# Halving the tails of a four-network graph kernel: fourth network in halves, jump bias and row bits moved into the layers, idle products at the seams

## The reference, cut to what matters

```python
# first network: attention
h = relu(layernorm(x)); s = si[:, :, None] + sj[:, None, :] + a_b
e = exp(s) * adj; x += einsum('bij,bjc->bic', e / e.sum(2), h)
# second network: rows are thinned one after another, then three layers
adj_d = dilate(adj, mask)
def sage(x, Wr, Wx, b):
    out = (einsum('bij,bjd->bid', adj_d, x) / deg) @ Wr + x @ Wx + b
    return out / max(norm(out), 1e-12)
h1 = bn(relu(sage(h, ...)));  h2 = bn(relu(sage(h1, ...)));  h3 = bn(relu(sage(h2, ...)))
x += (concat(h1, h2, h3) * mf) @ Wl + bl      # jump, with the bias bl
# "fourth network" in the words of the change: normalised adjacency
h = relu(layernorm(x)); x += einsum('bnm,bmo->bno', d * (adj + I) * d, h @ W2) + bias
# last network
h = relu(layernorm(x)); x += relu(einsum('bji,bjd->bid', adj > 0, h) @ U / deg)
```

## Time and profile before

| | us |
|---|---|
| median of 3 runs | 1387.33 (1386.73 to 1391.0) |
| the profiled execution | 1389.99 |
| its span, first to last instruction | 1388.3 |
| mean granted TensorE clock | 0.924 |
| PE busy | 1176.5 (85%) |
| DVE busy | 814.0 (59%) |
| ACT busy | 614.8 (44%) |
| POOL busy | 83.1 (6%) |

### The profile page before, as it was taken

One profiled execution on the slowest core, in us unless ns is written; L12 is line 12 of the kernel. 1 busy time (PEld: TensorE's weight loads), 2 busy tenths in 40 slices (PEclk: granted clock), 3 DMA queues, 4 the chain that ended last, 5 costly groups with the idle time before them and its releaser, 6 DMA issues. The chain is left out here.

```text
span 1388.3 us, 28432 instructions
## 1 busy us (share of the span) xinstructions
PE 1176.5 (85%) x10649; PEld 1028.9 (74%) x10649; DVE 814.0 (59%) x2816; ACT 614.8 (44%) x1510; POOL 83.1 (6%) x64
## 2 busy tenths in 40 slices
PE   4798879886488989988959999599997299998998
PEld 4798856554367777777859999599997298987554
DVE  4799577778755555565532343334454457766883
ACT  5699637766644444554222323313333223222541
POOL 2012000000000000000000000000000324310000
PEclk9899989975599999999979999799999589999999
DMA  9866000000045654456304563136675235671931
GB/s 324 284 245 243 32 2 3 2 3 2 2 182 215 240 220 188 187 200 239 123 31 166 199 242 123 44 146 228 237 296 226 85 120 223 264 275 77 409 119 46
DMA packets 75950, 225.35 MB, mean 162 GB/s; under 512 B 4960, under 2 KB 23584, under 8 KB 75808
## 3 DMA queue, kind: packets, MB, share of 16 engines
q1 hardware_dynamic: 75088, 223.40, 42.7%
q10 hardware_dynamic: 720, 0.07, 0.0%
HBM read 185.70 MB, written 37.75 MB: 161 GB/s over the span
## 5 line engine op out<-in xcount | busy, mean ns | idle before, releaser
L1332 PE MATMUL lay_acc<-lay_z,k_keepadj 128*128 128x128 f32 x1024 | 117.0, 275 | 0.0
L1332 PE MATMUL lay_acc<-lay_z,k_otheradj 128*128 128x128 f32 x1024 | 116.6, 275 | 0.0
L1332 PEld LDWEIGHTS lay_acc<-lay_z,k_keepadj 128*128 128x128 f32 x1024 | 115.6, 192 | 0.0
L1332 PEld LDWEIGHTS lay_acc<-lay_z,k_otheradj 128*128 128x128 f32 x1024 | 115.5, 192 | 0.0
L1416 DVE TENSOR_TENSOR lay_o<-lay_ring,k_vec 128x512 f32<-128x512 f32 x32 | 22.1, 692 | 135.3 <-PE lay_ring L1325 135.3
L1371 ACT ACTIVATE lay_junk<-lay_o 128x128 bf16<-128x128 f32 x128 | 37.7, 295 | 136.2 <-DVEq L1439 136.2
L1081 ACT ACTIVATE fuse_dist<-fuse_prank,k_kb 128x512 f16<-128x512 f32 (+2 forms) x96 | 55.3, 576 | 76.4 <-PE fuse_prank L974 73.0
L319 PE MATMUL att_acc<-att_rhs,att_adjT 128*128 128x130 f32 x512 | 63.2, 290 | 17.5 <-DMA att_adjT<-in_adj_cols 11.3
L319 PEld LDWEIGHTS att_acc<-att_rhs,att_adjT 128*128 128x128 f32 x512 | 62.5, 205 | 18.1 <-POOLq L276 18.1
L974 PE MATMUL fuse_prank<-k_fore,k_T 128*128 128x128 fp8e5 (+3 forms) x416 | 63.4, 291 | 11.0 <-PEq L140 7.5
L319 PE MATMUL att_acc<-att_rhs,k_keepadj 128*128 128x130 f32 x512 | 61.7, 285 | 7.9 <-DVEq L429 3.3
(11 more groups left out here) (268 smaller groups left out, 2623.2 us busy)
## 6 DMA issues: line engine op xcount, KB each, us to landing
k_keepadj<-in_adj_cols SPq DMA_DIRECT2D x28, 1024.0 KB, 8.1
k_keepadj<-keptT SPq DMA_DIRECT2D x12, 2048.0 KB, 10.5
k_otheradj<-keptT SPq DMA_DIRECT2D x12, 2048.0 KB, 11.5
att_adjT<-in_adj_cols SPq DMA_DIRECT2D x16, 1024.0 KB, 6.7
k_otheradj<-in_adj_cols SPq DMA_DIRECT2D x16, 1024.0 KB, 10.6
keptT<-k_keepadj SPq DMA_DIRECT2D x16, 1024.0 KB, 5.1
keptT<-k_otheradj SPq DMA_DIRECT2D x16, 1024.0 KB, 4.4
k_keepadj<-in_adj_cols SPq DMA_DIRECT2D x8, 2048.0 KB, 10.9
```

Source lines behind the costliest of these rows:

```text
L1332: mm = t.matmul(acc[i % 2][k][:, ib % HB, :], adjT[i % 2][:, jb, ib * P:(ib + 1) * P], zz[i % 2][:, jb, :], start=(jb == 0), stop=(jb == N ...
```

## The change

What it does, in the order of the phases:

- Attention: one semaphore per graph's features. The features of the third and fourth graph are loaded behind the first and second adjacency.
- Keep stage and layers: `outputs`, `squares`, `weights`, `rectified`, the transposes and (in the layers) the statistics work by halves of four tiles; the semaphores count halves.
- Layers: for the last graph, the transposes of the graph before stand between the two halves of its sums, not behind them. Behind the last sums the chain of the last graph runs half by half.
- Idle products (`keep_busy`): products of a 128x128 bf16 by a 128x512 fp8 operand whose result nobody reads, 26 at the end of the keep stage, 12 at the start and 18 at the end of each layer, 12 and 22 at the start of the fourth network.
- Row bits are made in layers 1 and 2; the fourth network has none.
- The jump bias is added by GpSimd in layer 2, two tiles at a time.
- Fourth network: `eT` for the entry beside `hT`; entry, projections, update, statistics, scales, normalisation, transposes, turned copies and support in halves; the degrees behind the first normalisation; `entry(b + 2)` ahead of the turned copy.

```diff
-ROWS_OF_LAYER = {1: [], 2: [(g, jb) for g in (0, 1) for jb in range(8)], 3: [(g, jb) for g in (2, 3) for jb in range(8)]}
+ROWS_OF_LAYER = {1: [(g, jb) for g in (0, 1) for jb in range(8)], 2: [(g, jb) for g in (2, 3) for jb in range(8)]}
@@ attention_phase
-                    sp.dma_start(x_rows(i), graph(A["x"], order[i])).then_inc(x_first[i] if i < 2 else x_rest, 16)
+                    sp.dma_start(x_rows(i), graph(A["x"], order[i])).then_inc(x_loaded[i], 16)
...
                 for i in range(2):
                     for c in range(NC):
                         load_adjacency(i, c)
-                for i in range(2, B):
+                    load_x(i + 2)
+                for i in range(4, B):
                     load_x(i)
@@ fuse_phase
+                    if b == B:
+                        keep_busy(t, K, pmask[0][:], 26)
...
-                def squares(b):
-                    act.wait_ge(out_ready, b + 1)
-                    for ib in range(NB):
+                def squares(b, half):
+                    act.wait_ge(out_ready, b * 2 + half + 1)
+                    for ib in range(half * HB, (half + 1) * HB):
...
+                        if ib == HB - 1:
+                            dve.drain().then_inc(out_ready, 1)
...
+def keep_busy(t, K, out, count):
+
+    for _ in range(count):
+        t.matmul(out, K["ident16"][:], K["fore8"][:, 0:HALF], start=True, stop=True)
@@ layer_phase, TensorE
+                keep_busy(t, K, acc[1][1][:].rearrange("p e d -> p (e d)"), 12)
...
+                    if i == B - 1:
+                        project(i - 1, "r0")
+                        project(i - 1, "r1")
                     if i < B:
                         sums(i, 1)
                         pe.drain().then_inc(adj_used, 1)
-                    if i > 0:
+                    if i == B:
+                        project(i - 1, "r0")
+                        pe.wait_ge(acc_free, B - 1)
+                        keep_busy(t, K, acc[B % 2][0][:].rearrange("p e d -> p (e d)"), 18)
+                        project(i - 1, "r1")
+                    elif 0 < i < B - 1:
@@ layer_phase, ScalarE
+                    if i == B:
+                        for half in range(2):
+                            squares(i - 1, half)
+                            rectified(i - 1, half)
+                            turned_copy(i - 1, half)
@@ layer_phase, GpSimd and VectorE
+                for i in range(B if final else 0):
+                    pool.wait_ge(x_added, 2 * i + 2)
+                    for tile in range(seq[i] * NB, (seq[i] + 1) * NB, 2):
+                        x = K["X"][:, tile:tile + 2, :]
+                        g.tensor_tensor(bl[:], along_tiles(K["vec"][:, V_BL, :], 2), along_features(K["mask"][:, tile:tile + 2], D),
+                                        ALU.mult)
+                        pool.drain()
+                        g.tensor_tensor(x, x, bl[:], ALU.add)
+                        pool.drain()
...
+                    if i == B:
+                        for half in range(2):
+                            outputs(i - 1, half)
+                            weights(i - 1, half)
+                        for half in range(2):
+                            batch_statistics(i - 1, half)
@@ gcn_phase, TensorE
+                keep_busy(t, K, tp[:, 0:HALF], 12)
                 project(0, 0)
-                turn(0)
+                keep_busy(t, K, acc[1][:].rearrange("p e d -> p (e d)"), 22)
+                turn(0, 0)
+                turn(0, 1)
                 project(0, 1)
@@ gcn_phase, ScalarE
+                entry(0)
+                for b in range(B):
+                    normalise(b)
                     if b == 0:
-                        act.wait_ge(sem["cols_ready"], 1)
-                    else:
-                        act.wait_ge(sem["pr_ready"], b * 2)
...
+                        act.wait_ge(deg_ready, 1)
+                        a.activation(dinv[:], dw[:, 1, :], ACT.Sqrt).then_inc(dinv_ready, 1)
+                    if b > 0 and b + 1 < B:
+                        entry(b + 1)
+                    turned_copy(b)
+                    if b == 0:
+                        entry(1)
@@ gcn_phase, VectorE
+                def normalise(b):
+
+                    update(b, 0)
+                    means(b, 0)
+                    update(b, 1)
+                    scales(b, 0)
+                    means(b, 1)
+                    scales(b, 1)
...
+                normalise(0)
+                degrees()
+                support(0)
+                for b in range(B):
+                    if b + 1 < B:
                         normalise(b + 1)
```

More of the change, by code:

```diff
@@ L1586, in body @@
-                    if not last:
+                        pe.wait_ge(loaded[b % 2], 32 * (b // 2))
+                    if b > 0:
+                        pe.wait_ge(sums_read, 2 * b - 1)
+                    sums(b, range(0, 4)).then_inc(sums_ready, 1)
+                    if b > 0:
+                        pe.wait_ge(sums_read, 2 * b)
+                    sums(b, range(4, 6))
+                    if b + 1 < B:
+                        turn(b + 1, 0)
+                        turn(b + 1, 1)
+                    sums(b, range(6, 8)).then_inc(sums_ready, 1)
@@ L1611, in body, with entry @@
-                def body(b, par, last):
-                    if not last:
-                        prepare(b + 1)
-                prepare(0)
-                for b in range(B):
-                    body(b, b % 2, b == B - 1)
-                norm_root(nc, act, K, w, B)
-                norm_apply(nc, act, lambda t: K["X"][:, t, :], h[:], w, B, sem["h_ready"])
+                def entry(b):
+                    for half in range(2):
+                        if b == 0:
+                            act.wait_ge(cols_ready, 1)
+                        else:
+                            act.wait_ge(pr_ready, projected(b - 1, 0, half))
+                        sl = slice(half * HALF, (half + 1) * HALF)
+                        a.activation(eT[:, sl], turned(T8, b)[:, sl], ACT.Identity, scale=c["col"][:, 4:5], bias=c["col"][:, 5:6])\
+                            .then_inc(eT_ready, 1)
@@ new lines, in normalise @@
+                def normalise(b):
+                    s_ = w["stat"]
+                    for half in range(2):
+                        ts = of_half(half)
+                        act.wait_ge(w["mean_ready"], 2 * b + half + 1)
+                        a.activation(s_[:, 0, ts], w["pair"][:, ts, 1], ACT.Sqrt, bias=K["eps"][:, 0:1]).then_inc(w["std_ready"], 1)
+                        act.wait_ge(w["scale_ready"], 2 * b + half + 1)
+                        for t in range(half * HB, (half + 1) * HB):
+                            last = a.activation(h[:, t, :], K["X"][:, b * NB + t, :], ACT.Relu, bias=s_[:, 2, t:t + 1],
+                                                scale=s_[:, 1, t:t + 1])
+                        last.then_inc(h_ready, 1)
```

374 lines of the change are left out of this document (179 added, 195 removed).

## The result

The median is **1349.66 us** (1348.63 to 1351.07, 4 runs) against 1388.39 (1386.73 to 1391.0, 4 runs) for the kernel before beside it: ratio 0.971, 95% interval 0.9692 to 0.9728. The profiled execution took 1351.07 us with a span of 1349.4; before it was 1389.99 and 1388.3. So 38.9 us went, where the forecast had 51.1. Cut at the same events in both traces, the span falls into these stretches (us). An aggregate is VectorE's instruction that makes mean and variance out of the statistics, the first one behind a seam; the sums are the products with the adjacency.

The account below looks back on a forecast made before the run. TensorE bounds the layers' insides (busy 99%); at five seams every instruction counts. 5.4 + 3 + 3.2 + 3.9 + 8.4 + 19.5 + 7.7 = 51.1 us off 1389.99 gave 1338.9, on the median's scale 1336; range 1322 to 1350.

Parts of the forecast that it names:

- rival 1: Idle products don't keep the clock: the 12 at three starts run slow, 1347, chance 0.12; all 120 slow, 1364, chance 0.03.
- Attention, 5.4: Attention stage: a semaphore per feature load ends VectorE's 13.06 us wait, third graph's products start near 59.4; 5.4 us gained.
- Keep stage, 3 + 3.2: Keep stage: working in halves gains 3 us inside and 3.2 us at its end, where 26 idle products fit.
- Starts, 2.5 + 1.4: Starts of layers 1 and 2: 12 idle products keep the full clock for the first products; 2.5 and 1.4 us gained.
- Layer ends, 4.2 + 4.2: Ends of both layers: transposes between the halves of the last sums, and a tail of one half; 4.2 us each.
- Rival 3: Layer 2: GpSimd's 4.2 us per graph holds VectorE on the path in all eight graphs, 34 us: 1370, chance 0.02.
- Moved work: Row compares one layer forward and jump bias to GpSimd in layer 2: 0 cost; row compares 10 us if uncovered.
- Fourth network, 19.5 + 7.7: Fourth network: its start in halves gains 19.5 us; a separate eT shortens the period per graph, 7.7 us in all.
- two stretches at 1.2 GHz: Fourth network's start: lower bound of the gain, 15 us instead of 19.5, if two stretches run at the low clock.
- Rival 2: Layer ends: turned rows come late and hold TensorE with half its sums open, so nothing is gained: 1344, chance 0.08.
- rival 4: Attention and keep stage: edits don't do what they say, 2.5 and 0 instead of 5.4 and 3: 1342, chance 0.12.
- rival 5: Slower overall: all 120 idle products uncovered at 1.2 GHz, 50.4 us on TensorE's path: 1391.7, chance 0.01.

Follow-up runs that it names:

- the eight: Eight profiles of kernels with the changed kernel's attention stage: the stretch to the removal stage's first counts took 157.88 to 160.78 us, mean 159.6.
- the late constants: Changed kernel with SyncE issuing the attention's 20 small constant transfers behind the fourth graph's adjacency instead of ahead of the third: 1341.78 us, ratio 0.9638.

## Why the prediction was right or wrong

The forecast was 1336, the range 1322 to 1350; the result, 1349.66, lies 0.3 us inside its upper end, and that it lies inside is luck: the same kernel once more had 1350.08. It is nearer to rival 1's 1347, which had a chance of 0.12, than to the forecast. The side and the seams held, and so did most prices; 12 of 51 us did not come, in four terms.

1. **Attention, 5.4.** Measured 3.6 in the first profile, 4.5 against the mean of the eight, and undoing the features' part cost 4.8 by the medians. The size was about right, the path to it was not. The 13 us wait went, but "SyncE ... reaches that load at 48.0 as before" came out as 49.51, and "its products start near 59.4 instead of 61.90" as 64.21, 2.3 us later than before instead of 2.5 earlier. The fourth adjacency, whose buffer the same edit frees earlier, was issued at 52.03 instead of 57.33; from 54 to 64 us the transfers moved 401 to 426 GB/s, so the third's 4 MB did not have that rate to themselves. That this sharing makes up the rest of the delay is argued, not tested. What did hold is that VectorE and ScalarE carry their shift to the end: their exponentials for the fifth graph start 3.1 us earlier (88.45 against 91.55), and the seventh graph's products 3.6 (126.17 against 129.81). What was late next I named, SyncE's constants, without asking what they cost: about 9 us, the largest single item the experiments found.
2. **Keep stage, 3 + 3.2.** Measured 2.8 and 3.5; over all kernels with this code the first lies between 0.8 and 3.3, so its size isn't settled. The 26 products took 5.78 us and fitted.
3. **Starts, 2.5 + 1.4.** Measured 0.0 and 0.1. The step that failed is "the 12 idle products (2.5 us) lie in the 2.8 us": rival 1's mechanism held at all three starts, for the 12 alone. Its price was too high in the layers: it took the slow products as lateness on top (2.5 each), but they only took the slow time over from the projection behind them (3.79 us before, 2.20 after). Its 1347 counted 11.4 us; six more products in front of the barriers won back 2.1, 1.4 and 2.6, so 6.1 was there to lose. The Trainium skill, TensorE: Matmul & The Clock Gate, "What's actually happening", has the throttled state as the default that activity releases. The 5.28 us for 12 products behind 2.23 us of quiet and the 2.75 behind 0.93 agree. The 2.75 behind 2.15 at one start of the kernel with the turns behind the sums shows that such a quiet does not always end in the slow state.
4. **Layer ends, 4.2 + 4.2.** Measured 3.6 and 0.6. In layer 1 the wait and turns took 3.4 us against 3.3 in the forecast and the tail 7.3 against 6.9. In layer 2 the step that failed is in "Moved work": GpSimd "collides with the next entry and a compare, 7 us before their products are wanted. 0". It also collided with the second compare and the weights of the graph before, which at the last graph are on the path: 1.3 us more wait, and then a second half at the low clock, 1.4 us. Rival 3 had this mechanism and priced it on all eight graphs (34 us); it counts at the last one, 2.9 us. The Trainium skill, SBUF — State Buffer, "Who interferes with whom", says that a `tensor_scalar` which can use both of VectorE's port pairs, and a `tensor_tensor` with both inputs in SBUF, contend with GpSimd. The compares' 1.83 instead of 1.29 us and the weights' 0.57 and 0.52 instead of 0.16 agree.
5. **Fourth network, 19.5 + 7.7.** Measured 16.5 and 7.9. Of the missing 3 us 2.6 are the 12 slow products and the slow second turn and projection; with the clock kept the start takes 16.43 us against 16 in the forecast, and VectorE's step beside GpSimd, which the forecast did not have, can account for the other 0.4 (not tested). The lower bound of 15, "two stretches at 1.2 GHz", was the case that came.
6. **Moved work otherwise.** Row compares in layer 1 cost TensorE nothing: from its first sums to those of the last graph 146.0 us before and after.
7. **Rival 2** fell (5.2 us the other way), **rival 4** did not come in the attention (how much the keep stage gave isn't settled), **rival 5** was far off: all 120 products together are worth 3.3 us by the stretches.

What stays open: why the attention stage differs by 1.7 us between two executions of one kernel (2.9 over the eight profiles), where the late constants' 9 us go under the old feature wait, and what GpSimd's addition costs at the fourth network's start. Leaving the jump bias out altogether was not tried.

## What to carry to other kernels

Filler for the clock belongs in front of the wait as well as behind it: six products before a barrier did what twelve behind it could not. The price is small all the same: the whole change's 120 were worth 3.3 us. When an edit removes a wait, follow the queue that feeds the next consumer to its end: here a wait on VectorE hid a queue of small transfers on SyncE that was worth about twice as much, and neither shows its full price while the other stands. Work moved onto an "idle" engine must be placed against the one iteration whose neighbours are on the critical path, here the last.

## What the runs showed of the hardware

- The same quiet does not always cost the clock. After waits of 1.8 and 0.54 us it stayed at 1.00 in one kernel and fell to 0.50 in another, 1.6 us apart; the same 12 products behind the same 2.15 us of quiet took 4.09 to 5.28 us in most executions and 2.75 at layer 2's start in the kernel with the turns behind the sums (there the 10 us in front had a clock of 0.75, in the changed kernel 1.00). Behind 0.85 to 0.93 us they took 2.75 at all six starts.
- GpSimd's two-tile additions (0.61 and 0.73 us alone) stretched even VectorE's 128x4 operations from 0.16 to 0.57 and 0.52 us, and were stretched themselves to 0.88 and 1.07. In the fourth network its 2.36 us addition took a 128x64 operation from 0.23 to 2.28.
- SyncE was held for 0.43 us by most of the small transfers, by one weight for 2.1: the 21 from the mask on took from 36.07 to 49.38, and a 4 MB load whose buffer was free by 37.8 (as the late constants showed) waited behind them.
